# Cross-attention with layer norm in float32: another order of the stages of a step, and low parts and transposes split otherwise

## The chip, the cores and the metric

The kernel runs on one core of a Trainium2 chip. A core has a matrix engine (TensorE, PE in the rows), VectorE (DVE), ScalarE (ACT), GpSimd (POOL) and SyncE (SP), which issues the transfers. Each takes its own instructions in the order in which they are written and waits on semaphores for the others. The metric is the time of the whole launch on the device, in microseconds (us); lower is better.

## What is computed

```python
Q = (img_embed @ Wq).reshape(B, -1, H, D).transpose(0, 2, 1, 3)
K = (sent_embed @ Wk).reshape(B, -1, H, D).transpose(0, 2, 1, 3)
V = (sent_embed @ Wv).reshape(B, -1, H, D).transpose(0, 2, 1, 3)
score = jnp.einsum('bhqd,bhkd->bhqk', Q, K) / math.sqrt(D)
mask = (atten_mask != 0)[:, None, None, :]
score = jnp.where(mask, score, -jnp.inf)
attn = jax.nn.softmax(score, axis=-1)
ctx = jnp.einsum('bhqk,bhkd->bqhd', attn, V).reshape(B, -1, H * D)
out = ctx @ Wo + img_embed
mu = jnp.mean(out, axis=-1, keepdims=True)
var = jnp.var(out, axis=-1, keepdims=True)
return (out - mu) * jax.lax.rsqrt(var + EPS) * gamma + beta
```

There are B = 8 batches, H = 8 heads of D = 256, 256 queries of width 256 and 256 keys of width DL = 192. All of it is float32.

## The kernel before

The weights are folded first: A = Wq Wk^T and C = Wv Wo for each head, so that a head needs only g = A^T x^T (query), scores = g ctx^T, softmax, t = p ctx (context) and out += t C (output). The width 192 is split in 128 "lower" columns (tiles whose names end in L) and 64 "upper" ones (U), and the upper parts of two heads share one tile. Each float32 operand is split into a high and a low part (`_hi`, `_lo`) of the type that the matrix engine takes at full rate, and a product is the sum of hi·hi, hi·lo and lo·hi. The high part is a copy by ScalarE, the low part a subtraction by VectorE or GpSimd.

A **step** t (0 to 31) is one pair of heads j = t mod 4 of batch b = t // 4. The steps 6 to 29 are a hardware loop of six turns of four steps (j = 2, 3, 0, 1); the others are written out. What an engine does in a step stands in its function `step`, and that order is fixed by hand:

- TensorE: `scores(t)` (20 matrix multiplications), `context_products(t-3)` (10 of twice the width), `query_products(t+1)` (18), `output_products(t-3)` (18, of which 12 lower and 6 upper; the upper six wait for the low part of tU).
- ScalarE: four exponentials of step t; `t_hi_part(t-3)` (tL_hi and two moves of halves of tU); the high parts of gU for step t+1; tU_hi; gL_hi; at j = 2 xT_hi and the high parts of the context; two pT_hi of step t-2.
- VectorE: `maxima(t)` (the negated scores and their minimum, two instructions for each head), the two `inverse_sum`, tL_lo, `tU_sum`, gU_lo, tU_lo, gU_lo, gL_lo, then the transposes of the probabilities in squares of 32 (four of 128x256), and at j = 2 the low parts of the context (`ctx_lo_part`). At j = 3 it adds the residual of the batch before and takes its statistics, at j = 0 it centres and normalises it.
- GpSimd: `normalise_probs` (one 128x512 product for each head), low parts of xT and ctxT, and the two pT_lo of step t-2.
- SyncE: `carry_squares` writes the squares to a scratch tensor and reads them back transposed as pT_raw; between these it loads the next batch.

The names hh = 0 and 1 mean the first and the second head of a pair. `inverse_sum(t, 1)` waits for the fourth exponential, and `normalise_probs` of a head for its inverse sum.

## Time and profile before

| what | value |
|---|---|
| median of 3 runs | 345.07 us (345.03 to 345.51) |
| span of the profiled execution, first to last instruction | 343.4 us |
| PE busy | 324.1 us (94%) |
| PE weight loads busy | 297.7 us (87%) |
| DVE busy | 272.4 us (79%) |
| ACT busy | 224.4 us (65%) |
| POOL busy | 175.5 us (51%) |
| mean granted TensorE clock | 0.996 |

A busy share is an average over the whole span; matrix multiplications overlap, so the busy time of PE counts less than what its queue needs. Times in the rows further on are microseconds from the start of the span, of that one execution. The 1.7 us between its span and the median lie outside the first and the last instruction.

### The profile page before, as it was taken

The numbers are of one execution on the slowest core, as the hardware profiler recorded it, in microseconds if no ns is written. First come the engines' busy times: TensorE is split into PE (matmuls) and PEld (weight loads), VectorE is DVE, ScalarE is ACT, GpSimd is POOL, SyncE is SP. The second block draws the span as 40 slices with busy tenths as digits, with TensorE's granted clock in tenths as the row PEclk, the third lists the DMA queues.
The fourth block names the chain that finished last, engine by engine and source line by source line (L and its number), as shares of the span: only waits on it lengthen the run. The fifth ranks groups of instructions, "written<-read, shape, count | busy, mean of one in ns | idle before, by whom it ended". The sixth has DMA issues, their size and how long they took to land.

```text
span 343.4 us, 7424 instructions
## 1 busy us (share of the span) xinstructions
PE 324.1 (94%) x2264; PEld 297.7 (87%) x2264; DVE 272.4 (79%) x797; ACT 224.4 (65%) x601; POOL 175.5 (51%) x167
## 2 busy tenths in 40 slices
PE   8999999998999989998999989998999989999993
PEld 6998889997989979898989979898989979898882
DVE  0468866779897798789997798879997798877685
ACT  2465677666767767566777767576777667666750
POOL 1132356554845467445745467446745567445601
PEclk9999999999999999999999999999999999999998
DMA  7995423363354542463354532553254532532100
GB/s 268 359 401 178 138 104 116 119 190 124 96 174 135 187 147 80 166 199 122 84 183 131 189 125 86 178 199 122 84 165 137 194 118 95 183 122 62 31 31 31
DMA packets 46911, 50.26 MB, mean 146 GB/s; under 512 B 3505, under 2 KB 37041, under 8 KB 46897
## 3 DMA queue, kind: packets, MB, share of 16 engines
q1 hardware_dynamic: 46608, 49.56, 43.7%
q10 hardware_dynamic: 288, 0.52, 0.6%
q8 instruction: 7, 0.11, 0.2%
q14 instruction: 8, 0.06, 0.0%
HBM read 32.24 MB, written 17.83 MB: 146 GB/s over the span
## 4 chain that ended last, share of the span: by engine, by line
PE 71%; DVE 12%; issue 10%; ACT 3%; DMA 2%; SPq 0%; DVEq 0%; POOLq 0%; ACTq 0%; POOL 0%
PE score_bank L342 19%; PE out_bank L342 16%; PE tL_bank L342 11%; PE gL_bank L342 8%; PE tU_bank L342 6%; PE gU_bank L342 4%; DVE ctxU L726 2%; DVE squares L808 2%; DMA wq_raw<-in_wqT 2%; DVE y_scaled L863 2%; DVE y_out L870 1%; DVE tL_lo L726 1%; DVE tU L836 1%; PE tL_bank L376 1%; PE spare_bank L376 1%
## 5 line engine op out<-in xcount | busy, mean ns | idle before, releaser
L610 ACT ACTIVATE probs<-neg_scores,neg_max 128x256 f32<-128x256 f32 x128 | 64.3, 504 | 66.1 <-DVE neg_max L787 63.9
L1032 POOL TENSOR_TENSOR pT_lo<-pT_raw,pT_hi 128x512 fp32r<-128x512 f32 x60 | 77.5, 1313 | 54.3 <-ACT pT_hi L565 54.3
L1009 POOL TENSOR_TENSOR probs<-probs,inv_sum 128x512 f32<-128x512 f32 x64 | 68.2, 1079 | 60.6 <-DVE inv_sum L798 60.0
L787 DVE CUSTOM_DVE_ANT_0 neg_scores<-score_bank,mask_bias 128x256 f32<-128x256 f32 x128 | 48.5, 420 | 12.6 <-PE score_bank L342 8.4
L808 DVE STREAM_TRANSPOSE squares<-probs 128x256 f32<-128x256 f32 x120 | 42.4, 411 | 0.0
L342 PE MATMUL score_bank<-ctxT_hi,gU 128*128 128x256 f32 x128 | 36.6, 286 | 0.0
L342 PE MATMUL out_bank<-CL_hi,tL_hi 128*128 128x256 f32 x118 | 33.9, 287 | 2.8 <-DVE tL_lo L726 2.8
L342 PE MATMUL score_bank<-ctxT_hi,gL_lo 128*128 128x256 f32 x128 | 36.3, 284 | 0.0
L342 PE MATMUL score_bank<-ctxT_hi,gL_hi 128*128 128x256 f32 x128 | 36.3, 283 | 0.0
L342 PE MATMUL score_bank<-ctxT_lo,gL_hi 128*128 128x256 f32 x128 | 36.2, 283 | 0.0
L342 PE MATMUL score_bank<-ctxT_lo,gU 128*128 128x256 f32 x128 | 36.1, 282 | 0.0
L342 PE MATMUL gL_bank<-xT_hi,A_hi 128*128 128x256 f32 x128 | 35.7, 279 | 0.0
L342 PE MATMUL gL_bank<-xT_lo,A_hi 128*128 128x256 f32 x128 | 35.7, 279 | 0.0
L342 PE MATMUL gL_bank<-xT_hi,A_lo 128*128 128x256 f32 x128 | 35.7, 279 | 0.0
L565 ACT ACTIVATE pT_hi<-pT_raw 128x512 fp32r<-128x512 f32 x60 | 34.3, 622 | 0.0
L342 PE MATMUL tL_bank<-pT_hi,ctxL_hi 128*128 128x512 f32 x62 | 25.1, 405 | 8.7 <-DVE ctxU L726 8.2
L342 PE MATMUL out_bank<-CL_hi,tL_lo 128*128 128x256 f32 x118 | 33.2, 282 | 0.0
L342 PE MATMUL out_bank<-CL_lo,tL_hi 128*128 128x256 f32 x118 | 33.2, 281 | 0.0
L726 DVE TENSOR_TENSOR tL_lo<-tL_bank,tL_hi 128x512 fp32r<-128x512 f32 x31 | 21.3, 687 | 11.4 <-ACT tL_hi L565 11.4
L726 DVE TENSOR_TENSOR gU<-gU_bank,gU 64x256 fp32r<-64x256 f32 x64 | 27.0, 422 | 2.3
L836 DVE TENSOR_TENSOR tU<-tU_bank,tU_moved 64x256 f32<-64x256 f32 x62 | 26.1, 421 | 3.2 <-ACT tU_moved L653 0.2
L342 PEld LDWEIGHTS out_bank<-CL_hi,tL_hi 128*128 128x128 f32 x118 | 22.2, 188 | 4.1 <-DVE tL_lo L726 4.0
(170 smaller groups left out, 959.5 us busy)
## 6 DMA issues: line engine op xcount, KB each, us to landing
scratch<-squares SPq DMA_DIRECT2D x30, 512.0 KB, 2.6
pT_raw<-scratch SPq DMA_DIRECT2D x120, 128.0 KB, 3.1
xT_raw<-in_xT SPq DMA_DIRECT2D x8, 256.0 KB, 3.0
ctxT_raw<-in_ctxT SPq DMA_DIRECT2D x8, 256.0 KB, 3.2
wo_raw<-in_wo SPq DMA_DIRECT2D x4, 512.0 KB, 13.1
x_res<-in_x SPq DMA_DIRECT2D x8, 256.0 KB, 3.3
out<-y_out SPq DMA_DIRECT2D x7, 256.0 KB, 3.0
wq_raw<-in_wqT SPq DMA_DIRECT2D x3, 512.0 KB, 7.5
```

Of the source, the lines that this page charges most:

```text
L342: ins = nc.tensor.matmul(into, stationary, moving, start=first and n == 0, stop=last and n == len(pairs) - 1, skip_group_check=shared)
L376: ins = nc.tensor.matmul(lower[:, hh, :], wv_raw[:, h * DT + d, 0:P], wo_raw[:, h * DT + d, :], start=d == 0, stop=d == DT - 1)
L565: return nc.scalar.activation(dst, src, ACT.Copy)
L610: nc.scalar.activation(probs[j % 2][:, n, :], neg_scores[:, n, :], ACT.Exp, bias=neg_max[:, n:n + 1], scale=-1.0, accum_out=row_sum[:, n:n ...
L726: return nc.vector.tensor_tensor(dst, whole, hi.bitcast(F32), ALU.subtract)
L787: nc.vector.tensor_tensor_reduce(out=neg_scores[:, n, :], in0=score_bank[hh][:, q, :], in1=mask_bias[:], scale=-SCALE, scalar=3.0e38, op0= ...
L808: nc.vector.transpose(squares[:, :, n, :], probs[j % 2][:, n, :].rearrange("p (s c) -> p s c", c=SQ)) \
L836: nc.vector.tensor_tensor(tU[part, :], places("tU", t)[0][part, hh, :], tU_moved[part, :], ALU.add).then_inc(tU_summed, 1)
L863: nc.vector.scalar_tensor_tensor(y_scaled[:, q, :], y[:, q, :], mean_var[:, q, 0:1], gamma_sb[:], ALU.subtract, ALU.mult).then_inc(y_scale ...
L870: nc.vector.scalar_tensor_tensor(y_out[:, q, :], y_scaled[:, q, :], rstd[:, q:q + 1], beta_sb[:], ALU.mult, ALU.add).then_inc(y_out_done, 1)
L1009: nc.gpsimd.tensor_tensor(probs[j % 2][:, rows, :], probs[j % 2][:, rows, :], inv, ALU.mult) \
L1032: nc.gpsimd.tensor_tensor(pT_lo[:, k].rearrange("p hh (q i r) -> p (hh q) i r", q=QT, i=ROWS), pT_raw[j % 2][:, k].rearrange("p i n r -> p ...
```

## The change

Nothing of the arithmetic changes. The parts are:

- TensorE's step becomes `scores(t)`, `query_products(t+1)`, `output_products(t-4)`, `context_products(t-3)`: the output of a step comes one step later, and the query products come right behind the scores.
- pT_hi and pT_lo exist twice, taken in turn by the parity of the step.
- ScalarE takes the high parts of t of step t-4 ahead of the exponentials, and tU_hi between the exponentials of the first and of the second head. The high parts of the context move from j = 2 to j = 3.
- VectorE takes tL_lo ahead of the maxima, tU_sum behind them, tU_lo behind the second inverse sum (and behind `finish_mask` at j = 3), and one transpose for each head (128x512 each) instead of four behind gL_lo: the first ahead of the low parts of g, the second behind them. Residual and statistics come at the end of step j = 3.
- The low parts of the context go to GpSimd, at j = 3, ahead of `normalise_probs`. `deviation` moves from j = 3 to the front of j = 0.
- SyncE carries the squares of j = 3 ahead of the load of the next context, and those of j = 0 ahead of the store of the result.
- Behind the loop, step 31 is written as scores, `output_products(27)`, `context_products(28)`; before, the context of step 28 stood between the scores of its two heads.

```diff
             def step(t, j, b, folds=()):          # tensor
                 scores(t, j, b)
-                if before:
-                    context_products(t - LAG, jb, bb)
                 query_products(t + 1, ja, ba)
-                if before:
-                    output_products(t - LAG, jb, bb)
+                if not (isinstance(t, int) and t < OUT_LAG):
+                    output_products(t - OUT_LAG, j, b - 1)
+                if not (isinstance(t, int) and t < LAG):
+                    context_products(t - LAG, jb, bb)
...
-            scores(STEPS - 1, 3, B - 1, heads=[0])
+            scores(STEPS - 1, 3, B - 1)
+            output_products(STEPS - 5, 3, B - 2)
             context_products(STEPS - 4, 0, B - 1)
-            scores(STEPS - 1, 3, B - 1, heads=[1])
...
             def step(t, j, b, folds=()):          # scalar
-                exponentials(t, j)
                 if before:
-                    t_hi_part(t - LAG)
+                    t_hi_part(t - OUT_LAG)
+                if j == PAIRS - 1:
+                    ctx_hi_part(b)
+                exponentials(t, j, heads=[0])
+                if before:
+                    tU_hi_part(t - OUT_LAG)
+                exponentials(t, j, heads=[1])
...
             def step(t, j, b, ends=None, folds=()):   # vector
+                if before:
+                    t_lo_part_lower(t - OUT_LAG)
                 maxima(t, b)
+                if before:
+                    tU_sum(t - OUT_LAG)
                 inverse_sum(t, 0)
                 if ends is not None and j == 0:
                     centre(ends)
                 inverse_sum(t, 1)
                 if j == 3:
                     finish_mask(b + 1)
                 if before:
-                    t_lo_part_lower(t - LAG)
-                    tU_sum(t - LAG)
+                    t_lo_part_upper(t - OUT_LAG)
+                if ends is not None and j == 0:
+                    normalise(ends)
+                if by_squares:
+                    transpose_squares(t, j, 0)
                 gU_lo_part(t + 1, 0)
-                if before:
-                    t_lo_part_upper(t - LAG)
                 gU_lo_part(t + 1, 1)
                 gL_lo_part(t + 1)
                 if by_squares:
-                    transpose_squares(t, j)
-                if j == 2:
-                    ctx_lo_part(b)
+                    transpose_squares(t, j, 1)
...
             def step(t, j, b, ends=None):         # gpsimd
+                if ends is not None:
+                    deviation(ends)
+                if j == PAIRS - 1:
+                    ctx_lo_part(b)
                 normalise_probs(t, j)
                 if j == PAIRS - 1 and not (isinstance(b, int) and b == B - 1):
                     ctxT_lo_part(b + 1)
-                if ends is not None:
-                    deviation(ends)
```

How the instructions stand in a row. ScalarE in step 30 (j = 2), the first behind the loop; in the loop the order is the same. Before:

```order
L610 ACTIVATE probs,row_sum<-neg_scores,neg_max 128x256 x4
L565 ACTIVATE tL_hi<-tL_bank 128x512
L652 ACTIVATE tU_moved<-tU_bank 64x256
L653 ACTIVATE tU_moved<-tU_bank 64x256
L565 ACTIVATE gU<-gU_bank 64x256 x2
L565 ACTIVATE tU_hi<-tU 128x256
L565 ACTIVATE gL_hi<-gL_bank 128x512
```

ScalarE, the same step now (`probs` are the exponentials):

```order
L528 ACTIVATE tL_hi<-tL_bank 128x512
L609 ACTIVATE tU_moved<-tU_bank 64x256
L610 ACTIVATE tU_moved<-tU_bank 64x256
L571 ACTIVATE probs,row_sum<-neg_scores,neg_max 128x256 x2
L528 ACTIVATE tU_hi<-tU 128x256
L571 ACTIVATE probs,row_sum<-neg_scores,neg_max 128x256 x2
L528 ACTIVATE gU<-gU_bank 64x256 x2
L528 ACTIVATE gL_hi<-gL_bank 128x512
```

tU_hi stands between the exponentials of the two heads, where it stood behind all four and the two gU.

VectorE in step j = 3 of the loop, from `finish_mask` (mask_bias) on, before:

```order
L756 REGISTER_ALU
L757 TENSOR_SCALAR mask_bias<-mask_low 128x256 [waits mask_lowered]
L825 ISA
L726 TENSOR_TENSOR tL_lo<-tL_bank,tL_hi 128x512 [waits t_hi_done]
L834 REGISTER_ALU
L836 TENSOR_TENSOR tU<-tU_bank,tU_moved 64x256 [waits tU_share_moved]
```

VectorE in the same step now, from the inverse sum of the second head (inv_sum) on:

```order
L748 RECIPROCAL inv_sum<-row_sum 128x2 [waits exp_done]
L713 REGISTER_ALU
L714 TENSOR_SCALAR mask_bias<-mask_low 128x256 [waits mask_lowered]
L685 TENSOR_TENSOR tU_lo<-tU,tU_hi 128x256 [waits t_hi_done]
L754 REGISTER_ALU
L758 STREAM_TRANSPOSE squares<-probs 128x2x8x32 [waits probs_done,squares_stored]
L718 ISA
L685 TENSOR_TENSOR gU<-gU_bank,gU 64x256 [waits g_hi_done]
```

Between mask_bias and the low part of tU stood tL_lo, both tU sums and a low part of gU; now tU_lo follows mask_bias at once, and the first transpose stands ahead of the low parts of g.

VectorE in step j = 0 of the loop, from centring (y_scaled) on, before:

```order
L863 SCALAR_TENSOR_TENSOR y_scaled<-y,mean_var,gamma_sb 128x256
L797 REGISTER_ALU
L798 RECIPROCAL inv_sum<-row_sum 128x2 [waits exp_done]
L870 SCALAR_TENSOR_TENSOR y_out<-y_scaled,rstd,beta_sb 128x256 [waits y_scaled_done,out_stored,rstd_done]
L870 SCALAR_TENSOR_TENSOR y_out<-y_scaled,rstd,beta_sb 128x256 [waits y_scaled_done]
L825 ISA
L726 TENSOR_TENSOR tL_lo<-tL_bank,tL_hi 128x512 [waits t_hi_done]
```

The same place now:

```order
L812 SCALAR_TENSOR_TENSOR y_scaled<-y,mean_var,gamma_sb 128x256
L747 REGISTER_ALU
L748 RECIPROCAL inv_sum<-row_sum 128x2 [waits exp_done]
L685 TENSOR_TENSOR tU_lo<-tU,tU_hi 128x256 [waits t_hi_done]
L819 SCALAR_TENSOR_TENSOR y_out<-y_scaled,rstd,beta_sb 128x256 [waits y_scaled_done,out_stored,rstd_done]
L819 SCALAR_TENSOR_TENSOR y_out<-y_scaled,rstd,beta_sb 128x256 [waits y_scaled_done]
L754 REGISTER_ALU
L758 STREAM_TRANSPOSE squares<-probs 128x2x8x32 [waits probs_done,squares_stored]
```

tU_lo stands ahead of the normalisation (y_out) and tL_lo is no longer behind it.

## Rows read from the trace of the kernel before

**Rows 1.** Who waited for whom, PE: us in total, times, longest us

```profile
PE tL_bank L342 <- DVE ctxU L726: 8.2, 6, 1.4
```

**Rows 2.** Chain of work that ended last: start us, us, what

```profile
162.62 1.20 PE tL_bank L342 x4
...
201.54 1.20 PE tL_bank L342 x4
...
218.69 2.40 PE score_bank L342 x20
...
223.41 0.71 PE gU_bank L342 x6
...
225.53 2.16 PE out_bank L342 x18
227.69 2.40 PE score_bank L342 x20
```

**Rows 3.** Timeline of step j = 1: start us, us, instruction [idle before <- releaser]

```profile
218.53 0.29 PE L342 MATMUL score_bank<-ctxT_hi,gU 128*128 128x256 f32 x1
...
221.29 0.43 DVE L787 CUSTOM_DVE_ANT_0 neg_scores<-score_bank,mask_bias 128x256 f32<-128x256 f32 x1 [0.42 <-PE score_bank L342]
...
221.98 0.16 DVE L798 RECIPROCAL inv_sum<-row_sum 128x2 f32<-128x2 f32 x1
222.89 0.17 DVE L798 RECIPROCAL inv_sum<-row_sum 128x2 f32<-128x2 f32 x1 [0.75 <-ACT probs L610]
...
224.66 0.88 DVE L836 TENSOR_TENSOR tU<-tU_bank,tU_moved 64x256 f32<-64x256 f32 x2
...
221.75 0.51 ACT L610 ACTIVATE probs<-neg_scores,neg_max 128x256 f32<-128x256 f32 x1
...
225.57 0.42 ACT L565 ACTIVATE tU_hi<-tU 128x256 fp32r<-128x256 f32 x1
```

**Rows 4.** Timeline of the last steps, ACT, DVE and PE

```profile
320.88 0.42 ACT L565 ACTIVATE tU_hi<-tU 128x256 fp32r<-128x256 f32 x1 [0.94 <-DVE tU L836]
321.20 1.14 ACT L565 ACTIVATE pT_hi<-pT_raw 128x512 fp32r<-128x512 f32 x2
...
336.04 0.42 DVE L726 TENSOR_TENSOR tU_lo<-tU,tU_hi 128x256 fp32r<-128x256 f32 x1 [0.49 <-ACT tU_hi L565]
...
336.52 0.39 PE L342 MATMUL out_bank<-CU_hi,tU_hi 128*128 128x256 f32 x1 [0.38 <-DVE tU_lo L726]
```

**Rows 5.** Timeline of step j = 0, centring on DVE beside the products on POOL

```profile
211.99 0.16 DVE L798 RECIPROCAL inv_sum<-row_sum 128x2 f32<-128x2 f32 x1
212.06 0.46 DVE L863 SCALAR_TENSOR_TENSOR y_scaled<-y,mean_var,gamma_sb 128x256 f32<-128x256 f32 x1
...
212.45 1.26 DVE L863 SCALAR_TENSOR_TENSOR y_scaled<-y,mean_var,gamma_sb 128x256 f32<-128x256 f32 x1
...
212.23 1.20 POOL L1009 TENSOR_TENSOR probs<-probs,inv_sum 128x512 f32<-128x512 f32 x1 [1.22 <-DVE inv_sum L798]
```

**Rows 6.** Timeline of step j = 3, DVE and POOL

```profile
204.53 0.29 DVE L757 TENSOR_SCALAR mask_bias<-mask_low 128x256 f32<-128x256 f32 x1
...
207.17 0.50 DVE L726 TENSOR_TENSOR tU_lo<-tU,tU_hi 128x256 fp32r<-128x256 f32 x1 [0.43 <-ACT tU_hi L565]
...
206.10 1.29 POOL L1021 TENSOR_TENSOR ctxT_lo<-ctxT_raw,ctxT_hi 128x512 fp32r<-128x512 f32 x1 [0.38 <-ACT ctxT_hi L565]
```

**Rows 7.** Timeline, the four transposes of a step on DVE

```profile
218.75 1.41 DVE L808 STREAM_TRANSPOSE squares<-probs 128x256 f32<-128x256 f32 x4
```

**Rows 8.** Timeline of step j = 1, POOL

```profile
227.21 2.55 POOL L1032 TENSOR_TENSOR pT_lo<-pT_raw,pT_hi 128x512 fp32r<-128x512 f32 x2 [2.95 <-ACT pT_hi L565]
```

**Rows 9.** Chain of work, scores of step 4

```profile
53.97 2.40 PE score_bank L342 x20
```

**Rows 10.** Timelines: POOL in step 3, PE in step 31

```profile
48.20 2.09 POOL L1009 TENSOR_TENSOR probs<-probs,inv_sum 128x512 f32<-128x512 f32 x2
...
316.14 0.47 PE L342 MATMUL tL_bank<-pT_hi,ctxL_hi 128*128 128x512 f32 x1 [0.46 <-issue]
```

More of the change, by code:

```diff
@@ L36 @@
 LAG = 3
+OUT_LAG = LAG + 1
 SQ = 32
@@ L111, in attention_kernel @@
         pT_raw = [sb(f"pT_raw{n}", [P, KT, ROWS, 2 * QT, SQ]) for n in range(2)]
-        pT_hi = sb("pT_hi", [P, KT, 2, S], F32R)
-        pT_lo = sb("pT_lo", [P, KT, 2, S], F32R)
+        pT_hi = [sb(f"pT_hi{n}", [P, KT, 2, S], F32R) for n in range(2)]
+        pT_lo = [sb(f"pT_lo{n}", [P, KT, 2, S], F32R) for n in range(2)]
         tL_hi = sb("tL_hi", [P, 2, S], F32R)
@@ L147, in places @@
             if not (isinstance(t, int) and t == STEPS - 2):
-                return {"pT": (pT_hi[:], pT_lo[:]),
-                        "tL": (tL_bank, tL_hi[:], tL_lo[:]),
+                return {"tL": (tL_bank, tL_hi[:], tL_lo[:]),
                         "tU": (tU_bank, tU_hi[:], tU_lo[:])}[name]
-            wide = [A[:, 0, 0:KT * 2 * S].rearrange("p (k hh s) -> p k hh s", k=KT, hh=2) for A in (A_hi, A_lo)]
-            return {"pT": (wide[0], wide[1]),
-                    "tL": (score_bank[0], xT_hi[:], xT_lo[:]),
+            return {"tL": (score_bank[0], xT_hi[:], xT_lo[:]),
                     "tU": (score_bank[1], gU[:, 0, :], gU[:, 1, :])}[name]
@@ L450, in context_products @@
                     pe.wait_ge(ctx_split, 2 * b + 2)
-                (hi, lo), tL, tU = places("pT", t), places("tL", t)[0], places("tU", t)[0]
+                hi, lo, tL, tU = pT_hi[j % 2], pT_lo[j % 2], places("tL", t)[0], places("tU", t)[0]
                 pe.wait_ge(pT_hi_done, 2 * t + 2)
@@ L509, in step @@
             def step(t, j, b, folds=()):
-                before = not (isinstance(t, int) and t < LAG)
                 jb, bb = (j - LAG) % PAIRS, b - 1 if j < LAG else b
@@ L660, in step @@
             def step(t, j, b, folds=()):
-                before = not (isinstance(t, int) and t < LAG)
-                exponentials(t, j)
+                before = not (isinstance(t, int) and t < OUT_LAG)
                 if before:
-                    t_hi_part(t - LAG)
+                    t_hi_part(t - OUT_LAG)
[5 more added lines that the diff above has]
+                exponentials(t, j, heads=[1])
                 if j == PAIRS - 1:
@@ L799, in inverse_sum, with transpose_squares @@
                                      row_sum[:, QT * hh:QT * hh + QT]).then_inc(inv_done, 1)
-            def transpose_squares(t, j):
-                if not (isinstance(t, int) and t == 0):
+            def transpose_squares(t, j, hh):
+                if hh == 0 and not (isinstance(t, int) and t == 0):
                     dve.wait_ge(squares_stored, 16 * t)
-                dve.wait_ge(probs_done, 2 * t + 2)
-                for n in range(2 * QT):
-                    nc.vector.transpose(squares[:, :, n, :],
-                                        probs[j % 2][:, n, :].rearrange("p (s c) -> p s c", c=SQ)) \
-                        .then_inc(squares_done, 1)
+                dve.wait_ge(probs_done, 2 * t + 1 + hh)
+                rows = slice(QT * hh, QT * hh + QT)
+                nc.vector.transpose(squares[:, :, rows, :].rearrange("p s n c -> p n s c"),
+                                    probs[j % 2][:, rows, :].rearrange("p n (s c) -> p n s c", c=SQ)) \
+                    .then_inc(squares_done, 1)
             def pT_lo_part(t):
@@ L915, in step @@
                 if by_squares:
-                    transpose_squares(t, j)
-                if j == 2:
-                    ctx_lo_part(b)
+                    transpose_squares(t, j, 1)
+                if ends is not None and j == 3:
+                    add_residual(ends)
+                    statistics(ends)
                 for pair in folds:
@@ L1032, in pT_lo_part, with ctx_lo_part @@
                     nc.gpsimd.tensor_tensor(
-                        pT_lo[:, k].rearrange("p hh (q i r) -> p (hh q) i r", q=QT, i=ROWS),
+                        pT_lo[j % 2][:, k].rearrange("p hh (q i r) -> p (hh q) i r", q=QT, i=ROWS),
                         pT_raw[j % 2][:, k].rearrange("p i n r -> p n i r"),
-                        pT_hi[:, k].rearrange("p hh (q i r) -> p (hh q) i r", q=QT, i=ROWS).bitcast(F32),
+                        pT_hi[j % 2][:, k].rearrange("p hh (q i r) -> p (hh q) i r", q=QT, i=ROWS).bitcast(F32),
                         ALU.subtract).then_inc(pT_split, 1)
+            def ctx_lo_part(b):
+                pool.wait_ge(ctx_hi_done, 2 * b + 2)
+                lower, upper = ctx_raw[:, :, 0:P], ctx_raw[:, :, P:DL]
+                lo_part(ctxL_lo[:], lower, ctxL_hi[:]).then_inc(ctx_split, 1)
+                lo_part(ctxU[:, :, UP:2 * UP], upper, ctxU[:, :, 0:UP]).then_inc(ctx_split, 1)
             def ctxT_lo_part(b):
@@ L1060, in _ @@
                 step(PAIRS * b + 2, 2, b)
-                step(PAIRS * b + 3, 3, b, ends=b - 1)
-                step(PAIRS * b + 4, 0, b + 1)
+                step(PAIRS * b + 3, 3, b)
+                step(PAIRS * b + 4, 0, b + 1, ends=b - 1)
                 step(PAIRS * b + 5, 1, b + 1)
             step(STEPS - 2, 2, B - 1)
-            normalise_probs(STEPS - 1, 3, heads=[0])
+            ctx_lo_part(B - 1)
+            normalise_probs(STEPS - 1, 3)
             pT_lo_part(STEPS - 3, 1)
-            normalise_probs(STEPS - 1, 3, heads=[1])
             deviation(B - 2)
```

58 lines of the change are left out of this document (24 added, 34 removed).

## The prediction

> **What bounds the kernel now.** I read first who waited for whom, because TensorE is busy nearly all the time and only its waits can be won. Its one large wait is for ctxU, the low part of the context on VectorE: 8.2 us in six times, once in each turn of the loop [rows 1]. Then the chain of work: the same place returns at 162.62 and 201.54, so a turn of four steps takes 38.92 [rows 2]. A step without any wait goes from 218.69 to 227.69, 9.00 us: scores 2.40, context 2.32 (223.41 less 218.69 and 2.40), query 2.12 (225.53 less 223.41), output 2.16 [rows 2]. Four of them are 36.00, so a turn holds 2.92 of waits, and six turns 17.5. The chain runs through TensorE except at these waits: TensorE's order is the bound, and the others matter where they make it wait.
>
> **What is removed.** The wait for ctxU goes: GpSimd makes that low part at the start of step j = 3, and the context products that need it now stand last in the step, 6.7 us behind its first score. Its price on GpSimd is in no row; the nearest is 1.29 for a low part of 128x512 [rows 6], which gives about 1.0 for the 128x256 and 128x128 by size. Even twice that fits before 6.7. The waits for tL_lo go too, since tL_lo has all of the scores and the query products for itself. So the whole 2.92 of a turn goes, 17.5 in all, and I have to ask what is late next.
>
> **What is added: tU_hi now waits for the maxima of the second head.** In VectorE's queue tU_sum stands behind all four maxima, ScalarE's second pair of exponentials stands behind tU_hi, the second inverse sum behind these, and tU_lo behind that; the six upper output products wait for tU_lo. From the first score (0) the timetable of a plain step is:
> - maxima of the second head start: 221.29 less 218.53, 2.76 [rows 3];
> - both done and the next instruction starts: 0.69 (to 221.98) [rows 3];
> - the two tU sums until tU_hi starts: 0.91 (224.66 to 225.57) [rows 3];
> - tU_hi until the next instruction of ScalarE starts: 0.32 (320.88 to 321.20) [rows 4];
> - two exponentials until the inverse sum starts: 1.14 (221.75 to 222.89) [rows 3];
> - to the next instruction of VectorE: 0.07 (211.99 to 212.06) [rows 5];
> - tU_lo until the product that waited for it starts: 0.48 (336.04 to 336.52) [rows 4].
>
> That is 6.37. TensorE comes there at 2.40 + 2.12 + 12/18 of 2.16 = 5.96. So it waits 0.41 in every plain step, and the first product behind a wait takes some 0.10 more (0.39 against 0.28 to 0.29) [rows 4, 3]: **0.51 a step**, where before there was none. Nothing hides it: the wait stands in TensorE's own queue, with the context products and the next scores behind it. The bounds of this term: 0.3 if tU_hi passes faster behind an exponential, 0.7 if ScalarE takes the full 0.42 of tU_hi and the maxima come later.
>
> **j = 3: tU_lo behind GpSimd.** [Rows 5] show what two inputs in on-chip memory cost VectorE beside GpSimd. The first y_scaled starts at 212.06 and takes 0.46; GpSimd's product starts at 212.23, takes 1.20 and ends 0.91 behind that y_scaled; the second starts at 212.45 and ends at 213.71, 0.28 behind GpSimd. One is stopped while the other runs. tU_lo is such an instruction: at 207.17 it ended 0.28 behind ctxT_lo of GpSimd (206.10 + 1.29) [rows 6]. At j = 3 finish_mask now stands between the inverse sum (5.82) and tU_lo. GpSimd's product of the second head starts 0.24 behind the inverse sum (211.99 to 212.23) [rows 5], so at 6.06; mask_bias starts at 5.89 and with its 0.29 [rows 6] holds until 6.18, tU_lo starts some 0.08 ahead of that end as the second y_scaled did, at 6.10, and GpSimd is already waiting. Then 6.18 + 0.91 + 0.28 = 7.37, and 0.06 to TensorE: 7.43, a wait of 1.47 and 0.10, **1.57** for this step.
>
> The Trainium skill, page "SBUF — State Buffer", section "Who interferes with whom", has this as a rule: a VectorE instruction with two SBUF inputs and a GpSimd instruction that reads SBUF exclude each other, and whoever starts first keeps the shared ports for all of its instruction. The trace agrees (0.46, 1.20 and 1.26 in [rows 5]). It speaks against moving tU_lo next to `normalise_probs`; without it the sum below would be 8.7 less.
>
> **j = 0: centring in between.** Inverse sum of the first head at 4.35, y_scaled 4.43 to 4.89, GpSimd to 5.80, the second y_scaled to 6.08, the second inverse sum at 6.00, tU_lo at 6.08, TensorE at 6.56: wait 0.60 and 0.10. GpSimd's second product then holds from 6.50 to 7.41, the first y_out ends at 7.69 and the second at 8.07. The transpose comes next. Its price as one 128x512 is in no row: four of 128x256 take 1.41 [rows 7], so it lies between 0.34 and 1.41; by columns it is some 0.65. With two gU_lo of 0.45 the scores of the next step can start at 9.6, needed at 9.70; gL_lo comes 0.1 late, with 0.1 for the restart. **0.90** for this step. In plain steps 1.5 us of slack stand behind tU_lo, so the transposes cost nothing there unless one takes over 1.4.
>
> **The sum.** A turn: 36.00 + 2 x 0.51 + 1.57 + 0.90 = 39.49 against 38.92, +0.57; six turns +3.4. Steps 4, 5 and 30 lie outside the loop: 3 x 0.51 = +1.5. Step 3 has no output yet and is short: GpSimd, free at 48.20 [rows 10], does the low parts of the context (1.0), both products (2.09) and ctxT_lo (1.29) until 52.6, and the scores of step 4 wait for the last. Before, they started at 53.97 [rows 9] with an output of 2.16 already done, so the same work stood at 51.8: +0.8 (bounds 0 and 1.5). Step 31 has no query products to cover the chain: 6.37 less 2.40 and 1.44 = 2.53, and 0.10. Its context is followed at once by what needs tL_lo and tU_lo, where half of the scores (1.20) stood between: up to 1.2 more, I take 1.1. The wait of 0.6 in step 31 (0.46 and a slow first product, 316.14) goes [rows 10]. Together +3.1 (bounds 2 and 4.5). Residual, statistics and SyncE's new order have 1.5 us and more of slack and cost nothing; if the statistics pushed the next maxima, it would be 0.1 a turn.
>
> 3.4 + 1.5 + 0.8 + 3.1 = +8.8. On the profiled span of 343.4 that is 352.2; the median lies 1.7 above that span, so **353.9**.
>
> **Rivals.**
> 1. At j = 0 the second y_out is stopped too, by pT_lo. ScalarE has tU_hi at 4.36, exponentials to 5.66, two gU_hi (about 0.78) and then gL_hi and pT_hi; from a tU_hi to pT_lo through these two it took 1.64 (225.57 to 227.21) of which 0.44 was tU_hi [rows 3, 8]. So pT_lo starts at 7.64; the second y_out starts at 7.61. That is a tie. If GpSimd gets in, y_out ends 1.05 later, and with the slack of 0.1 used up the turn grows by 1.0: +6.1, **360.0**.
> 2. VectorE keeps the ports between mask_bias and tU_lo at j = 3 (they are 0.08 apart). Then tU_lo starts at 6.10 and TensorE goes on at 6.58, 0.72 instead of 1.57: -5.1, **348.8**.
> 3. Neither stop occurs and only the chain of tU_hi is left: 4 x 0.51 a turn is 0.88 less than the 2.92 that go, six turns -5.3, and with the 5.4 outside the loop it is **345.2**, no change.
> 4. The other side: the chain is shorter than I have it. Outside the loop the change costs 5.4, so it pays as soon as a turn's waits fall below 2.92 - 0.90 = 2.02, half a microsecond a step. With no waits in the loop and in steps 4, 5 and 30 it would be 345.1 - 17.5 + 3.9 = **331.5**. For it: 0.41 of wait is a small difference of a sum of seven pieces, and tU_hi has not been seen between exponentials. Against it: each piece has its row, and the stops on the ports must be absent as well.
> 5. The transpose of 128x512 costs more than twice one of 128x256 (strided output). From 1.0 on it delays gL_lo in every turn: 0.5 us a turn at 1.0, some 358 and more.
>
> **How the numbers follow.** Forecast 353.9: 0.40. Rival 1: 0.23. Rival 2: 0.14. Rival 3: 0.09. Rival 4: 0.06. Rival 5: 0.08. A change of 0.2% (0.7 us) is about what a measurement of this kernel can tell from none. The forecast and rivals 1, 2 and 5 are slower, 0.85; rival 3 with its bounds of 0.1 a step lies on both sides and gives 0.03 to slower, 0.04 to same and 0.02 to faster; rival 4 is faster. So faster 0.08, same 0.04, slower 0.88. The range takes in rivals 1 and 2 with their bounds (0.51 a step may be 0.45 or 0.6, 1.7 to 2.5 over 28 steps): 346.5 to 362.0.
>
> **What would show it.** In the profile of the changed kernel the wait of PE for ctxU is gone, and a wait of out_bank for DVE tU_lo takes its place, some 27 times, 0.4 to 0.5 in plain steps and about 1.5 at j = 3. VectorE waits before the inverse sum for the exponentials, ScalarE before tU_hi for tU. The unstalled pieces of TensorE keep 2.40, 2.32, 2.12 and 2.16. tU_lo lasts about 1.2 us at j = 3, and one y_out is long (first y_out near 1.2; both long says rival 1). The forecast is wrong if PE waits for tU_lo in fewer than half of the steps, or if a turn of the loop takes less than 38.9.

## The result, and the profile after

The changed kernel takes **354.11 us** (median of 4 runs, 353.70 to 355.18) against 345.05 for the kernel before: a ratio of 1.027, 95% interval 1.025 to 1.028. It is slower. 353.9 was forecast. The profiled execution has a span of 351.9 us against 343.4, so 8.5 of the 9.1 us can be read from the two traces. The granted clock was 0.998 of full speed.

First the page of the kernel after, its part on busy time and its part on the chain that ended last (share of the span by engine):

```profile
PE 324.7 (92%) x2264; PEld 295.0 (84%) x2264; DVE 257.3 (73%) x721; ACT 219.4 (62%) x601; POOL 186.7 (53%) x183
...
PE 49%; DVE 25%; issue 12%; ACT 7%; POOL 2%; DMA 2%; DVEq 1%; ACTq 1%; SPq 0%; POOLq 0%
```

TensorE is still busy for 92% of the time, but only half of the chain runs through it; before, 71% did, with 12% on VectorE. The kernel became one in which TensorE is held by VectorE. Who waited for whom says where (engine, line, waited for: us in total, times, longest):

```profile
ACT tU_hi L528 <- DVE tU L785: 35.0, 31, 1.2
DVE inv_sum L748 <- ACT probs L571: 29.9, 26, 1.3
...
PE out_bank L312 <- DVE tU_lo L685: 18.7, 29, 2.4
...
PE score_bank L312 <- POOL ctxT_lo L970: 0.7, 1, 0.7
```

The wait for ctxU [rows 1] is gone and the one for tL_lo almost (0.4 once). In their place stands a new one, 29 times: the upper output products wait for tU_lo. The two rows above it are the links of the chain that the prediction added up: ScalarE waits for the tU sum, VectorE for the second exponentials.

One turn of the loop by TensorE's own timeline (start us, us, instruction [idle before <- releaser]): the first score of each step, and the first upper output product between them.

```profile
199.40 0.28 PE L312 MATMUL score_bank<-ctxT_hi,gU 128*128 128x256 f32 x1
...
206.80 0.38 PE L312 MATMUL out_bank<-CU_hi,tU_hi 128*128 128x256 f32 x1 [1.38 <-DVE tU_lo L685]
...
209.95 0.28 PE L312 MATMUL score_bank<-ctxT_hi,gU 128*128 128x256 f32 x1
...
216.47 0.39 PE L312 MATMUL out_bank<-CU_hi,tU_hi 128*128 128x256 f32 x1 [0.49 <-DVE tU_lo L685]
...
219.63 0.33 PE L312 MATMUL score_bank<-ctxT_hi,gU 128*128 128x256 f32 x1
...
226.25 0.39 PE L312 MATMUL out_bank<-CU_hi,tU_hi 128*128 128x256 f32 x1 [0.30 <-DVE tU_lo L685]
...
229.40 0.28 PE L312 MATMUL score_bank<-ctxT_hi,gU 128*128 128x256 f32 x1
...
238.87 0.28 PE L312 MATMUL score_bank<-ctxT_hi,gU 128*128 128x256 f32 x1
```

The steps take 10.55 (j = 3), 9.68 (j = 0), 9.77 (j = 1, with its first scores still slow from gU_lo and gL_lo) and 9.47 (j = 2): a turn of 39.47. Forecast were 39.49 against 38.92 before [rows 2].

The whole difference can be put together from two pairs of starts, the scores of step 4 and of step 31, first before, then after, and from the two spans:

```profile
53.80 0.28 PE L342 MATMUL score_bank<-ctxT_hi,gU 128*128 128x256 f32 x1
...
314.32 0.29 PE L342 MATMUL score_bank<-ctxT_hi,gU 128*128 128x256 f32 x1
```

```profile
52.39 0.39 PE L312 MATMUL score_bank<-ctxT_hi,gU 128*128 128x256 f32 x1 [0.67 <-POOL ctxT_lo L970]
...
317.85 0.28 PE L312 MATMUL score_bank<-ctxT_hi,gU 128*128 128x256 f32 x1
```

| stretch | before | after | difference | forecast |
|---|---|---|---|---|
| to the scores of step 4, with the output of 2.16 that is still owed after | 53.80 | 54.55 | +0.75 | +0.8 |
| from there to the scores of step 31 | 260.52 | 265.46 | +4.94 | +4.9 (six turns 3.4, steps 4, 5 and 30 1.5) |
| step 31 to the end, less the 2.16 owed | 29.08 | 31.89 | +2.81 | +3.1 |
| sum | 343.4 | 351.9 | +8.5 | +8.8 |

### The profile page after: what moved, and what is told of

It is laid out like the page before. It is cut to its first block, busy times and chain, and to the rows that moved or that the text cites. A ratio compares the mean times of both kernels' runs of the same rounds, so it can differ in the third digit from the quotient of the medians.

```text
span 351.9 us, 7399 instructions
## 1 busy us (share of the span) xinstructions
PE 324.7 (92%) x2264; PEld 295.0 (84%) x2264; DVE 257.3 (73%) x721; ACT 219.4 (62%) x601; POOL 186.7 (53%) x183
## 4 chain that ended last, share of the span: by engine, by line
PE 49%; DVE 25%; issue 12%; ACT 7%; POOL 2%; DMA 2%; DVEq 1%; ACTq 1%; SPq 0%; POOLq 0%
PE score_bank L312 18%; PE tL_bank L312 10%; PE out_bank L312 7%; DVE tU L785 6%; PE tU_bank L312 6%; DVE neg_scores L737 5%; ACT probs L571 5%; DVE tU_lo L685 4%; DVE y_scaled L812 3%; DMA wq_raw<-in_wqT 2%; PE gL_bank L312 2%; DVE squares L758 1%; PE tL_bank L346 1%; PE spare_bank L346 1%; DVE gU L685 1%
## 5 line engine op out<-in xcount | busy, mean ns | idle before, releaser
L958 POOL TENSOR_TENSOR probs<-probs,inv_sum 128x512 f32<-128x512 f32 x64 | 69.7, 1092 | 106.3 <-DVE inv_sum L748 106.3
L737 DVE CUSTOM_DVE_ANT_0 neg_scores<-score_bank,mask_bias 128x256 f32<-128x256 f32 x128 | 49.3, 422 | 16.5 <-PE score_bank L312 12.0
L528 ACT ACTIVATE tL_hi<-tL_bank 128x512 fp32r<-128x512 f32 x31 | 18.5, 598 | 43.6 <-PE tL_bank L312 43.6
L758 DVE STREAM_TRANSPOSE squares<-probs 128x512 f32<-128x512 f32 x60 | 42.1, 702 | 1.8 <-POOL probs L958 1.5
L312 PE MATMUL out_bank<-CU_hi,tU_hi 128*128 128x256 f32 x59 | 19.7, 334 | 18.8 <-DVE tU_lo L685 18.7
L528 ACT ACTIVATE tU_hi<-tU 128x256 fp32r<-128x256 f32 x31 | 13.0, 418 | 35.0 <-DVE tU L785 35.0
L748 DVE RECIPROCAL inv_sum<-row_sum 128x2 f32<-128x2 f32 x64 | 10.5, 164 | 30.8 <-ACT probs L571 29.9
```

Source lines behind the costliest of these rows:

```text
L312: ins = nc.tensor.matmul(into, stationary, moving, start=first and n == 0, stop=last and n == len(pairs) - 1, skip_group_check=shared)
L528: return nc.scalar.activation(dst, src, ACT.Copy)
L737: nc.vector.tensor_tensor_reduce(out=neg_scores[:, n, :], in0=score_bank[hh][:, q, :], in1=mask_bias[:], scale=-SCALE, scalar=3.0e38, op0= ...
L748: nc.vector.reciprocal(inv_sum[:, QT * hh:QT * hh + QT], row_sum[:, QT * hh:QT * hh + QT]).then_inc(inv_done, 1)
L758: nc.vector.transpose(squares[:, :, rows, :].rearrange("p s n c -> p n s c"), probs[j % 2][:, rows, :].rearrange("p n (s c) -> p n s c", c ...
L958: nc.gpsimd.tensor_tensor(probs[j % 2][:, rows, :], probs[j % 2][:, rows, :], inv, ALU.mult) \
```

## Experiments

Turns and steps below are read as above, from one start of a score product to the next. All times are medians; the kernel before, run beside them, took 344.9 to 345.2.

**1. finish_mask behind tU_lo.** Is the long wait at j = 3 really finish_mask letting GpSimd in?

```diff
-                if j == 3:
-                    finish_mask(b + 1)
                 if before:
                     t_lo_part_upper(t - OUT_LAG)
+                if j == 3:
+                    finish_mask(b + 1)
```

> The changed kernel, with finish_mask at j = 3 put behind tU_lo instead of ahead of it. Theory (finish_mask lets GpSimd's product in, and tU_lo is stopped by it): at j = 3 TensorE waits 0.3 us for tU_lo instead of 1.4, as in a plain step, and tU_lo lasts 0.40 instead of 1.26. Six steps of the loop, 1.08 each: -6.5 us, 347.6. Rival A (finish_mask costs only its own 0.29 on VectorE, and GpSimd gets in front of tU_lo all the same): -1.8 us, 352.3. Rival B (VectorE would just be late with the transposes behind it): no change, 354.

Measured: 354.12 us, no change of the median. By the time alone rival B had won. The trace says otherwise. VectorE and TensorE of this kernel in steps j = 3 and j = 0:

```profile
204.48 0.17 DVE L748 RECIPROCAL inv_sum<-row_sum 128x2 f32<-128x2 f32 x1 [1.27 <-ACT probs L571]
204.56 0.40 DVE L685 TENSOR_TENSOR tU_lo<-tU,tU_hi 128x256 fp32r<-128x256 f32 x1
204.89 1.13 DVE L714 TENSOR_SCALAR mask_bias<-mask_low 128x256 f32<-128x256 f32 x1
...
209.49 0.75 DVE L804 BATCH_NORM_STATS2 stats<-y 128x6 f32<-128x256 f32 x2
210.16 0.42 DVE L809 BATCH_NORM_AGGREGATE mean_var<-stats 128x2 f32<-128x6 f32 x2
210.52 0.69 DVE L685 TENSOR_TENSOR tL_lo<-tL_bank,tL_hi 128x512 fp32r<-128x512 f32 x1
211.13 0.41 DVE L737 CUSTOM_DVE_ANT_0 neg_scores<-score_bank,mask_bias 128x256 f32<-128x256 f32 x1
```

```profile
205.02 0.38 PE L312 MATMUL out_bank<-CU_hi,tU_hi 128*128 128x256 f32 x1 [0.30 <-DVE tU_lo L685]
...
215.58 0.39 PE L312 MATMUL out_bank<-CU_hi,tU_hi 128*128 128x256 f32 x1 [1.39 <-DVE tU_lo L685]
```

tU_lo takes 0.40 and the wait at j = 3 is 0.30: the stop is gone, and step j = 3 takes 9.47 instead of 10.55, as expected. (mask_bias is now the one that is stopped, 1.13 instead of 0.29.) But the wait of 1.39 is back one step later: j = 0 takes 10.55 instead of 9.68. VectorE still has the residual and the statistics in front of tL_lo. The maxima start 2.96 behind the first score (211.13 less 208.17, read from the same timeline) where they started 1.91 behind it in the changed kernel (211.86 less 209.95), and the chain of tU_lo hangs on them. Of the 1.08 won at j = 3, 0.87 was given back at j = 0, if this reading is right. The next pair tests it. The 0.21 a turn that is left (39.28 instead of 39.50, mean of six turns) is 1.3 us: the profiled execution took 352.37 where that of the changed kernel took 353.70, both at a granted clock of 0.998. The median does not show it, because the other four executions of this run had 0.993 to 0.994, and in the changed kernel only one of four had (see the clock, below).

**2 and 3. The residual and the statistics cut short, with finish_mask ahead of tU_lo and behind it.** Both kernels take 8 of 256 columns there, so their output lacks the rest; y is cleared once ahead of the loop.

```diff
-                nc.vector.tensor_tensor(y[:], out_bank[:], x_res[:], ALU.add)
+                nc.vector.tensor_tensor(y[:, :, 0:8], out_bank[:, :, 0:8], x_res[:, :, 0:8], ALU.add)
...
-                    nc.vector.bn_stats(stats[:, q, :], y[:, q, :])
+                    nc.vector.bn_stats(stats[:, q, :], y[:, q, 0:8])
```

> The changed kernel, with the residual sum and the statistics in the loop cut to 8 of 256 columns (the output lacks the rest; VectorE has about 1.2 us less to do at the end of step j = 3). It is the control for the next run. Theory: at j = 3 TensorE is held so long by the stopped tU_lo that VectorE is done with these before it is needed in step j = 0: no change, 354.1 (353.4 to 354.8). Rival (the statistics delay tL_lo and the maxima of j = 0 in the changed kernel too): -2 us or more.

> The same cut of the residual sum and the statistics, with finish_mask behind tU_lo. Theory (in mask_behind the 1.08 us that j = 3 won was given back at j = 0, because residual and statistics then hold tL_lo and the maxima there): now it is kept, a turn of 38.4 instead of 39.5, 354.1 - 6.3 = 347.8. Rival (what j = 3 wins is lost in some other place, such as pT_lo on GpSimd or the squares' round through memory): as mask_behind, 353 to 354.

Measured: 354.57 us (353.84 to 355.61) for the first and **348.19** us (347.36 to 349.04) for the second, whose turn takes 38.42. That settles both points. The statistics cost nothing in the changed kernel (a turn of 39.50 with them and without), because TensorE is held by the stopped tU_lo meanwhile; and the stop costs only 0.2 a turn as long as the statistics stand behind it. Either alone can be removed with little or no gain. Together they are worth 6 us.

**4. tU_lo ahead of the second inverse sum.** Is it the end of the chain (second exponentials, inverse sum) that binds?

```diff
+                if before:
+                    t_lo_part_upper(t - OUT_LAG)
                 inverse_sum(t, 1)
                 if j == 3:
                     finish_mask(b + 1)
-                if before:
-                    t_lo_part_upper(t - OUT_LAG)
```

> The changed kernel, with tU_lo put ahead of the second inverse sum on VectorE in every step, nothing else moved. Theory (the last links of the chain, two exponentials and the inverse sum between tU_hi and tU_lo, 1.1 us, make TensorE wait): the waits for tU_lo vanish in plain steps and at j = 3 (steps of 9.00), and stay at j = 0, where centring stands ahead. A turn of 36.9 instead of 39.5, six turns -15.4, three steps outside -1.4: 337.3. Rival (the wait for tU_lo covers another one, for pT_lo or gL_lo, that then shows): less than half of it, 346 or more.

Measured: 341.94 us (340.57 to 342.43). Most of the gain came; the waits for tU_lo in the loop vanish except at j = 0, where 0.53 is left. The expectation was 4.6 too low: a turn took 37.46, not 36.9, and plain steps 9.13, not 9.00, which is 0.20 more than an unstalled step of the new order (8.93, experiment 5). In its new place tU_lo runs beside GpSimd's product of the first head and is stopped by it. VectorE and GpSimd of one step:

```profile
225.43 1.11 DVE L685 TENSOR_TENSOR tU_lo<-tU,tU_hi 128x256 fp32r<-128x256 f32 x1
...
225.22 1.04 POOL L958 TENSOR_TENSOR probs<-probs,inv_sum 128x512 f32<-128x512 f32 x1 [3.54 <-DVE inv_sum L748]
```

The rest of the miss stands in the last steps (see the clock, below).

**5. The tU sum between the maxima, nothing else.** Is it the head of the chain?

```diff
-                maxima(t, b)
+                maxima(t, b, heads=[0])
                 if before:
                     tU_sum(t - OUT_LAG)
+                maxima(t, b, heads=[1])
                 inverse_sum(t, 0)
```

> The changed kernel, with VectorE's tU sum between the maxima of the two heads and nothing else moved: tU_lo stays behind the second inverse sum, finish_mask and centring. It tells the chain's length from what stands in front of tU_lo at its end. Theory: tU_hi follows the first exponentials, the second ones no longer wait for it, the second inverse sum is at 4.5 us from the first score, tU_lo at 4.6: plain steps have no wait (9.00). At j = 3 finish_mask still stands ahead and GpSimd's second product gets in: tU_lo ends at 6.5, a wait of 0.6; at j = 0 0.5 to 0.9 as before. A turn of 37.4, 340.3. Rival (the stop at j = 3 is worth nothing, as when finish_mask went behind tU_lo): a turn of 36.7 or less, 336.

Measured: 345.53 us (345.27 to 347.36), 5.2 above the expectation. The plain step had no wait (8.93), j = 3 waited 0.47, both as expected. At j = 0 a step of 10.51 appeared, 0.6 to 1.0 longer than expected. There VectorE, GpSimd and TensorE show the thing that rival 1 of the prediction describes:

```profile
210.24 2.69 DVE L819 SCALAR_TENSOR_TENSOR y_out<-y_scaled,rstd,beta_sb 128x256 f32<-128x256 f32 x2
...
210.07 1.14 POOL L959 TENSOR_TENSOR probs<-probs,inv_sum 128x512 f32<-128x512 f32 x1 [0.44 <-DVE inv_sum L748]
211.17 2.90 POOL L982 TENSOR_TENSOR pT_lo<-pT_raw,pT_hi 128x512 fp32r<-128x512 f32 x2
...
214.51 0.38 PE L312 MATMUL score_bank<-ctxT_hi,gU 128*128 128x256 f32 x1 [0.82 <-DVE gU L685]
```

The two y_out take 2.69 us: the first is stopped by GpSimd's product, the second by pT_lo, and gU_lo behind them is late for the next scores. The exponentials no longer wait for tU_hi, so pT_hi is done sooner, and pT_lo sooner with it: a faster ScalarE let GpSimd in ahead of VectorE. In the changed kernel the same two y_out take 1.66, and pT_lo starts 0.07 behind the second and is stopped itself (1.56 instead of 1.30):

```profile
217.52 0.48 DVE L819 SCALAR_TENSOR_TENSOR y_out<-y_scaled,rstd,beta_sb 128x256 f32<-128x256 f32 x1
...
217.59 1.56 POOL L981 TENSOR_TENSOR pT_lo<-pT_raw,pT_hi 128x512 fp32r<-128x512 f32 x1 [0.27 <-ACT pT_hi L528]
```

**6. The same, with y_out moved to j = 1** (the call of step j = 1 is given the batch to end). What is that second stop worth?

```diff
                 if ends is not None and j == 0:
                     centre(ends)
+                if ends is not None and j == 1:
+                    normalise(ends)
...
-                if ends is not None and j == 0:
-                    normalise(ends)
```

> As sum_only, with the two y_out instructions moved to step j = 1, between the inverse sums. In sum_only the second y_out ran into pT_lo of GpSimd (1.51 us instead of 0.4) and TensorE waited 0.82 for gU_lo, then for gL_lo. Theory (that stop costs a turn 1.5 us: 1.1 at j = 0 and 0.4 at j = 1): a turn of 36.9 instead of 38.4, 345.5 - 8.7 = 336.8. Rival (the squares, gU_lo and gL_lo of j = 0 are late for the centring alone): half of it or less, 341 or more.

Measured: 340.58 us (339.16 to 340.81), 5.0 less than sum_only. j = 0 fell from 10.51 to 9.53 and j = 1 from 9.28 to 9.16; a turn from 38.37 to 37.26. The move is worth about 1.1 a turn, not 1.5. Without y_out, j = 0 gains 0.98, and j = 1 gains 0.35 because its first scores no longer start late: 1.33, and the stop can be worth no more than that. But y_out has a price in its new place too: it stands ahead of the second inverse sum and of tU_lo, takes 1.64 there, and the upper output products of j = 1 start 0.15 late, the first of them slow. VectorE and TensorE's weight load of that step:

```profile
214.66 1.64 DVE L819 SCALAR_TENSOR_TENSOR y_out<-y_scaled,rstd,beta_sb 128x256 f32<-128x256 f32 x2
...
216.30 0.40 DVE L685 TENSOR_TENSOR tU_lo<-tU,tU_hi 128x256 fp32r<-128x256 f32 x1
...
216.76 0.19 PEld L312 LDWEIGHTS out_bank<-CU_hi,tU_hi 128*128 128x128 f32 x1 [0.20 <-DVE tU_lo L685]
```

That is the 0.23 of step j = 1. In experiment 9 tU_lo stands ahead of y_out, and it is gone. Of the 6.7 that six turns give, 1.7 are missing again in the time; the lower clock of the last steps (0.993 over this span, 0.998 in sum_only) is the difference that the page shows: step 31 to the end takes 35.57 instead of 34.04.

**7. Both ends of the chain.** The tU sum between the maxima as in 5, and tU_lo directly behind the first inverse sum, ahead of centring, mask and second inverse sum.

```diff
+                maxima(t, b, heads=[1])
                 inverse_sum(t, 0)
+                if before:
+                    t_lo_part_upper(t - OUT_LAG)
```

> The changed kernel, with VectorE's tU sum between the maxima of the two heads (tU_hi then follows the first exponentials at once) and tU_lo directly behind the first inverse sum, ahead of centring, of the second inverse sum and of finish_mask. Theory (only the chain through tU_sum, tU_hi, second exponentials, inverse sum, tU_lo binds, and the two instructions that stand between at j = 3 and j = 0): all waits for tU_lo in the loop vanish, a turn takes 36.0 to 36.2, 3.4 us less six times and 1.4 outside: 332.3. Rival A (the maxima of the second head, 0.9 us later, hold the second exponentials and so the transposes, gL_lo and the next scores): a wait of scores for gL_lo of 0.2 to 0.5 in every step, 338 to 346. Rival B (a wait for pT_lo on GpSimd was hidden): PE waits for pT_lo, 340 or more.

Measured: **333.81 us** (333.28 to 334.44); a ratio of 0.967 to the kernel before. TensorE never waits for tU_lo in the loop. A turn takes 36.30: 8.92 to 8.93 in plain steps, and 0.6 more in two steps, because gU_lo and gL_lo are late behind centring and y_out. So TensorE's new order was sound; VectorE's order behind it was what cost.

**8. The same in step 31.** There TensorE has no query products to cover the chain, and still waited 2.4 us.

```diff
-            maxima(STEPS - 1, B - 1)
+            maxima(STEPS - 1, B - 1, heads=[0])
             tU_sum(STEPS - 5)
+            maxima(STEPS - 1, B - 1, heads=[1])
             inverse_sum(STEPS - 1, 0)
-            inverse_sum(STEPS - 1, 1)
             t_lo_part_upper(STEPS - 5)
+            inverse_sum(STEPS - 1, 1)
```

> The changed kernel with tU sum between the maxima and tU_lo behind the first inverse sum in the loop, and now in step 31 as well, where TensorE still waits 2.4 us for tU_lo. Theory (that wait is the same chain, bare, since step 31 has no query products): tU_lo there is ready 1.5 to 1.9 us sooner, 333.8 - 1.7 = 332.1. Rival (the tail is bound by something else, the products and transposes of the last two steps): 333.8.

Measured: 331.21 us (330.87 to 331.38), 2.6 less. The wait fell from 2.38 to 0.37, by 2.0 and not by the 1.5 to 1.9 expected; for the rest see the clock below.

**9. And y_out at j = 1.** The edit of 6 on top of 8.

> As sum_tail, with the two y_out instructions of VectorE moved from step j = 0 to step j = 1, to the place between tU_lo and the second inverse sum. Theory (in step j = 0 centring, y_out and the statistics before them fill VectorE, so that gU_lo and gL_lo come 0.4 us late for the scores of j = 1): a turn of 36.0 instead of 36.3 to 36.4, -2 us against sum_tail, 330. Rival (GpSimd's products stop y_out in step j = 1 just as long and the same 0.4 is lost one step later): no change against sum_tail.

Measured: **327.65 us** (327.26 to 327.71), ratio 0.950 (0.948 to 0.951) to the kernel before: the fastest of all. A turn takes 35.70, four steps of 8.93, with no wait of TensorE left in the loop. Who waited for whom, TensorE, all of it from 0.4 us up, and the chain by engine:

```profile
PE tL_bank L328 <- DMA wq_raw<-in_wqT: 1.2, 1, 1.2
PE score_bank L491 <- POOL zeros L945: 1.1, 1, 1.1
PE out_bank L312 <- DVE tU_lo L685: 0.9, 2, 0.5
PE score_bank L312 <- POOL ctxT_lo L972: 0.7, 1, 0.7
PE out_bank L312 <- DVE tL_lo L685: 0.4, 1, 0.4
```

```profile
PE 88%; DVE 4%; POOL 2%; ACT 2%; DMA 2%; issue 1%; SPq 1%; POOLq 0%; DVEq 0%
```

**10. One part alone: the context's low parts on GpSimd, in the kernel before.**

First VectorE's step, then GpSimd's.

```diff
-                if j == 2:
-                    ctx_lo_part(b)
...
+                if j == 2:
+                    ctx_lo_part(b)
                 if not (isinstance(t, int) and t < LAG - 1):
                     pT_lo_part(t - LAG + 1, (j - LAG + 1) % PAIRS)
```

> The kernel before, with one part of the change alone: the low parts of the context (ctxL_lo and ctxU) are made by GpSimd in step j = 2, between xT_lo and pT_lo, instead of by VectorE at the end of that step. Theory (TensorE's order of the kernel before was not at fault, its one large wait was): the wait for ctxU, 8.2 us in six times, goes, with 0.1 of restart each: -8.8, 336.3; if VectorE, relieved of about 1 us at j = 2, also has tL_lo in time, 333.5. Rival (GpSimd is the next to be late: pT_lo ends 1.1 us later and TensorE waits for it inside the context products): -3 or less, 342 or more.

Measured: 337.84 us (337.74 to 337.92), ratio 0.979. This part alone makes the kernel before 7.2 us faster. The wait for ctxU is gone. The one for tL_lo stays as it was (2.8 before), and a small new one for pT_lo comes up:

```profile
PE out_bank L342 <- DVE tL_lo L726: 2.7, 6, 0.5
PE tL_bank L342 <- POOL pT_lo L1023: 1.4, 6, 0.2
```

The sum of the expectation, 336.3, left the second out; its rival named it, but at more than the 0.24 a turn that it is.

**11. One part alone: the squares transposed per head, in the kernel before** (two instructions of 128x512, each behind its own head's product).

> The kernel before, with one part of the change alone: the squares of a head are transposed by one instruction of 128x512, behind GpSimd's product of that head, instead of four of 128x256 behind both products. Theory: one 128x512 costs as much as two of 128x256 (0.70 in the changed kernel, two of them 1.40, against 1.41 for the four), and the path of the kernel before does not lead through them: no change, 345 within 0.7. Rival (they start earlier by one GpSimd product, ctxU stands directly behind them in step j = 2, so its wait of 1.37 shrinks by up to 0.5 in each turn): -1 to -3 us, 342 to 344.

Measured: 345.03 us, ratio 1.000 (0.999 to 1.001). This part does nothing. The wait for ctxU stays at 8.1 us in six times.

**12. One part undone: the context's low parts back on VectorE, in the fastest kernel.**

```diff
+                if j == 3:
+                    ctx_lo_part(b)
                 inverse_sum(t, 1)
...
             t_lo_part_upper(STEPS - 5)
+            ctx_lo_part(B - 1)
             inverse_sum(STEPS - 1, 1)
```

> As y_out_later, the fastest so far, with one part of the change undone: the low parts of the context go back to VectorE, in step j = 3 ahead of the second inverse sum. Theory (in the new order of TensorE the context products that need ctxU stand at the end of the step, so the wait for it is gone whoever makes it, and VectorE has 1.3 us to spare there): no wait of PE for ctxU, within 1 us of 327.7; step 3 may win up to 0.5 us, since ctxT_lo on GpSimd no longer stands behind it. Rival (the part was needed: on VectorE it is stopped by GpSimd's product, the second inverse sum comes 0.8 us later and with it the squares, gU_lo and gL_lo): scores of step j = 0 wait, +1 us a turn, 334.

Measured: 327.68 us (327.56 to 327.75), the same as 327.65. In the new order nobody waits for ctxU, whoever makes it. It is stopped by GpSimd (ctxL_lo takes 1.26), and the second inverse sum comes later, but both have room. In step 3 a wait of 0.47 us at the context products stands in place of 0.18 there and 0.67 for ctxT_lo, and that step is 0.54 shorter. Step 31 gives it back: its context products wait 0.45 for the same low part, and from step 31 to the end it takes 32.73 instead of 32.01. So the place of this part is worth half a microsecond or somewhat more at either end, in opposite directions, and nothing in the loop.

## Why the prediction was right, and where it was not

**The chain of a plain step, 0.51: measured 0.54.** The unstalled step of the new order is 8.93 (experiments 5 and 9), a stalled one 9.47. The forecast step was 9.51, since it took the query products at 2.12 where they run in 2.04 now (0.68 and 1.36 on the chain of experiment 7); why they run faster is not shown. The pieces, VectorE and ScalarE of step j = 1, and ahead of them the second head's maxima of step j = 2, which begins at 229.40:

```profile
232.15 0.42 DVE L737 CUSTOM_DVE_ANT_0 neg_scores<-score_bank,mask_bias 128x256 f32<-128x256 f32 x1 [0.42 <-PE score_bank L312]
...
223.37 0.87 DVE L785 TENSOR_TENSOR tU<-tU_bank,tU_moved 64x256 f32<-64x256 f32 x2
...
225.71 0.17 DVE L748 RECIPROCAL inv_sum<-row_sum 128x2 f32<-128x2 f32 x1 [1.27 <-ACT probs L571]
225.79 0.40 DVE L685 TENSOR_TENSOR tU_lo<-tU,tU_hi 128x256 fp32r<-128x256 f32 x1
...
224.28 0.42 ACT L528 ACTIVATE tU_hi<-tU 128x256 fp32r<-128x256 f32 x1 [1.23 <-DVE tU L785]
224.60 0.49 ACT L571 ACTIVATE probs<-neg_scores,neg_max 128x256 f32<-128x256 f32 x1
```

First score to the second head's maxima 2.75 (229.40 to 232.15), sum to tU_hi 0.91, tU_hi 0.32, exponentials to the inverse sum 1.11, inverse sum 0.08, tU_lo to TensorE 0.46 (225.79 to 226.25): and 0.69 for the two maxima (222.68 to 223.37). Each is within 0.03 of the number taken from the trace before. In step j = 2 the product that waits starts 6.32 behind the first score (forecast 6.37), and without the wait it would start at 5.86 (forecast 5.96, too late by the query products), so it starts 0.46 late and loses 0.1 more by being slow. The profile's own figure for this wait is 0.30 and not the 0.4 to 0.5 named as a sign, since it counts from the modelled end of the product before. Experiments 4, 5 and 7 show that these links are the cause: with the head of the chain cut (5) or both ends (7) no plain wait is left, with the end cut (4) 0.20.

**What was luck.** The forecast turn of 39.49 is within 0.02 of the measured one, but two misses cancel in it: the waits of a turn came to 3.75 and not 3.49, and four unstalled steps to 35.72 and not 36.00.

**j = 3, tU_lo behind GpSimd, 1.57: measured 1.62.** The step took 10.55, and tU_lo 1.26 us with finish_mask ahead of it:

```profile
205.28 0.29 DVE L714 TENSOR_SCALAR mask_bias<-mask_low 128x256 f32<-128x256 f32 x1
205.49 1.26 DVE L685 TENSOR_TENSOR tU_lo<-tU,tU_hi 128x256 fp32r<-128x256 f32 x1
...
205.42 1.04 POOL L958 TENSOR_TENSOR probs<-probs,inv_sum 128x512 f32<-128x512 f32 x1 [0.40 <-DVE inv_sum L748]
```

Rival 2, in which VectorE keeps the ports, did not occur in any of the six turns: all 31 tU_lo take 17.7 us together, which is 25 of 0.405 and 6 of 1.262. Experiment 1 moved the instruction and tU_lo fell to 0.40.

**j = 0, 0.90: measured 1.06**, 0.75 in the step itself and 0.31 at the next scores, for gL_lo and a little for gU_lo (step j = 1 of 9.77 to 9.80 against 9.47). Rival 1 did not occur here, by 0.07 us, and did in experiment 5: pT_lo starts 7.64 behind the first score, as the rival has it, and the second y_out at 7.57, where the rival has 7.61. The forecast rightly called it a tie and gave it 0.23.

**The transposes: a price that was wrong and did no harm.** I took 0.65 for one of 128x512. It is 0.70, and two of them cost what the four cost before [rows 7]:

```profile
L758 DVE STREAM_TRANSPOSE squares<-probs 128x512 f32<-128x512 f32 x60 | 42.1, 702 | 1.8 <-POOL probs L958 1.5
```

Rival 5 needed 1.0. Experiment 11 shows that even the earlier start brings nothing.

**Step 3 and the last steps, +0.8 and +3.1: measured +0.75 and +2.81** (the table). GpSimd made the context's low parts in 1.1 us where I took 1.0.

**Rivals 3 and 4** fell with the plain wait: it is there in every step. What decides is the waits of a turn: with 39.47 less 35.72 = 3.75 the change loses, with 2.65 (experiment 5) it is within 0.5 us of the kernel before, with 1.54 (experiment 6) it wins 4.3. The line drawn at about 2 was somewhat low: experiment 5 comes out even at 2.65, with the waits of steps 4, 5 and 30 gone as well.

**What I had wrong without paying for it:** that residual and statistics "have 1.5 us and more of slack and cost nothing". They cost nothing only because tU_lo was stopped just ahead of them. Without the stop they cost 0.9 a turn (experiments 1 to 3). Nor does the prediction say that the order of VectorE alone turned a gain of 17 us into a loss of 9.

## What to carry to other kernels

When a step's order is changed on the engine that bounds the kernel, write the chain behind it in the order of every queue that it passes, piece by piece from rows; here a third of a microsecond a step (9 us over 28 steps) decided the sign. Put what the bounding engine waits for directly behind its own input in each queue, ahead of what only has to be done some time in the step; here two such moves took 354 to 334 us. And an edit that frees a microsecond at one place and hardly changes the time has not been shown useless: look in the trace whether the next step got longer, and take both away together.
